# Second attention of a four-layer kernel: two PSUM banks for the products of maxima and three for those of exponents, in place of three and two

## The chip, the cores and the metric

The kernel runs on one core of one Trainium2 chip. The metric is the device time of one execution in microseconds. A core has TensorE (PE, whose weight loads have a row of their own, PEld), VectorE (DVE), ScalarE (ACT), GpSimd (POOL) and SyncE (SP, which only issues DMAs here). TensorE writes its results to PSUM, which this kernel uses as eight banks of 512 fp32 columns on 128 partitions; VectorE and ScalarE read them from there.

## What is computed

The input is x of shape (4, 512, 512). Four layers follow one another, each added to x: an attention with a learned sparse mask (`attn_a`), a feed-forward layer, a differential attention (`attn_b`), and the same feed-forward layer again. The change lies in `attn_b`, whose input is the layer-normed x:

```python
q1, k1, q2, k2 = ...            # (B, T, 16 heads, 16), slices of x @ W_attn
v = ...                         # (B, T, 16 heads, 32)
lam = exp(dot(lambda_q1, lambda_k1)) - exp(dot(lambda_q2, lambda_k2)) + LAMBDA_INIT
attn1 = einsum('bthd,bshd->bhts', q1, k1) * scale
attn2 = einsum('bthd,bshd->bhts', q2, k2) * scale
score = softmax(attn1 - lam * attn2, axis=-1)
out = einsum('bhts,bshd->bthd', score, v)
out = (1.0 - LAMBDA_INIT) * out.reshape(B, T, E)
return out @ W_proj
```

## The kernel before

The whole kernel is written by hand in Bass. Each engine has its own queue and runs it strictly in order; engines wait for one another through semaphores (`wait_ge`). The function `attention_b` (L1949) emits the second attention. It goes by 16 units (`UNITS`, L1826), each of four heads (`HU`) of one of four batches, four units to a batch. A unit has 16 tiles (`TILES`, L1827) of 128 rows by 512 columns.

The softmax is computed twice over. For the maxima, TensorE makes the product of a tile of 128 queries with all 512 keys (step `max_b`, L2117) into a bank of `O1_BANKS`, and VectorE reduces it to a maximum per query (L2220, `maxes_b`). When all 16 tiles of a unit are done, the maxima are transposed by TensorE (step `place_b`, L2124), copied by ScalarE (L2276) and placed by four DMAs as one more row of the stacked queries. For the exponents, TensorE then makes the transposed product, 128 keys by 512 queries, with the maximum already subtracted through that row (step `exp_b`, L2132), into a bank of `O2_BANKS`, and ScalarE takes its exponential (L2288, `ex_b`, a ring of ten buffers). GpSimd adds the exponentials of a unit up (L2070, `ex_sum`), in the last unit VectorE half of them. TensorE multiplies them with the values (step `weighted_b`, L2143, bank 5) and sums `ex_sum` over partitions (step `sums_b`, L2155). VectorE divides in eight pieces (step `divide_b`: a reciprocal, L2229, and a multiplication, L2230). The projection follows for each batch (step `project_b`, L2166, added to x in L2236).

Other steps run beside these through two side banks (6 and 7): the normed rows (`norm_b`, L2192) are transposed (`turn_b`, L2079, copied in L2255), and from these come values (`values_b`, L2090, copied in L2260) and queries and keys (`product_b`, L2102). The latter are split into a high half on ScalarE (L2270) and a low half on VectorE (L2212), and sent by SyncE through a DRAM buffer to the stacks (`send_b`, L2315 and L2319).

The order of all this is written out by `order_of_attention_b` (L1830), and every engine walks the same list and takes its own part of each step. It goes in slots: each holds one `exp_b` and one `max_b`, and behind these perhaps a `weighted_b` (every fourth), half of a side step, a `divide_b`, a `norm_b` or a `stats_b`. The exponents of unit n run `LAG` = 6 slots behind the maxima of unit n+1. A product of maxima waits until its bank has been read, and so does one of exponents:

```python
pe.wait_ge(max_made, i + 1 - len(O1_BANKS))   # L2116, i counts the tiles of maxima
pe.wait_ge(ex_made, i + 1 - len(O2_BANKS))    # L2131, i counts the tiles of exponents
```

The last batch is projected in steps `early_b` (L2178: three of four parts, as soon as there is a bank) and `last_b` (L2183), each of whose four tiles has a bank of `LAST_BANKS`; they are added to x in L2242. The first steps of the second feed-forward layer (`EARLY_FFN`, L1322) stand among them in the order. Its transposes (`turned`, L1497, banks 4 and 5) wait for all exponentials, and two of them stand ahead of the first `early_b` that the change touches.

Of the kernel before, what the change touches and what calls it, by code (L numbers as in the profile page):

```python
# [7 lines left out]
ACT = mybir.ActivationFunctionType  # L8
AX = mybir.AxisListType
# [6 lines left out]
P = 128  # L16
B, S, D = 4, 512, 512
NT = S // P
# [1930 lines left out]
def attention_b(k, mem):  # L1949
    nc, d, ps, x = k.nc, k.d, k.ps, k.x  # L1950
    pe, dve, act, pool, sp, chain = k.pe, k.dve, k.act, k.pool, k.sp, k.dve_chain
    signal = k.flag
    ROWS, N_EX, N_OUT, SCALE = 97, 10, UNITS_B + 1, HDB ** -0.5
    O1_BANKS, O2_BANKS, SUM_BANK, SIDE = (0, 1, 2), (3, 4), 5, (6, 7)
    LAST_BANKS = O1_BANKS + O2_BANKS[:1]
    order = order_of_attention_b()
    nth = numbered(order)
    small, qk_weights, v_weights, proj_weights = (
# [113 lines left out]
    def tensor(kind, *at):  # L2072
        step = (kind, *at)
        if kind == "turn_b":
            b, f = at
            pe.wait_ge(zb_made, NT * b + NT)
            side_free(step)
            for t in range(NT):
                s = nc.tensor.transpose(ps[:, side_bank[step], t * P:t * P + P], z[:, t, f * P:f * P + P],  # L2079
                                        k.ident[:, :])  # L2080
            s.then_inc(zb_turned, 1)
        elif kind == "values_b":
            b, t, half = at
            bank = side_bank[step[:3]]
            if half == 0:
                pe.wait_ge(zt_made, ND * b + ND)
                pe.wait_ge(v_weights, 16)
                side_free(step[:3])
            for f in range(2 * half, 2 * half + 2):
                s = nc.tensor.matmul(ps[:, bank, :], z_t[:, b % 2, f, t * P:t * P + P], w_v[:, f, :],  # L2090
                                     start=f == 0, stop=f == ND - 1)
            if half:
                s.then_inc(vb_done, 1)
        elif kind == "product_b":
            n, i, half = at
            b, c, bank = n // UNITS_B, n % UNITS_B, side_bank[step[:3]]
            if half == 0:
                pe.wait_ge(zt_made, ND * b + ND)
                pe.wait_ge(qk_weights, 16)
                side_free(step[:3])  # L2100
            for f in range(2 * half, 2 * half + 2):
                s = nc.tensor.matmul(ps[:, bank, :], w_qk[:, f, c, i, :], z_t[:, b % 2, f, :], start=f == 0,  # L2102
                                     stop=f == ND - 1)
            if half:
                s.then_inc(qk_done, 1)
        elif kind == "query_scale":
            pe.wait_ge(lam_made, 4)
            nc.tensor.matmul(ps[:, SUM_BANK, 0:1], q2_row[:, :], lam[:, 1:2], start=True,
                             stop=True).then_inc(lam_spread, 1)
        elif kind == "max_b":  # L2110
            n, j = at
            g, t = divmod(j, NT)
            i = TILES * n + j
            if j == 0:
                pe.wait_ge(stacked[n % 3], 16 * 6 * (n // 3 + 1))
            pe.wait_ge(max_made, i + 1 - len(O1_BANKS))  # L2116
            nc.tensor.matmul(ps[:, O1_BANKS[i % 3], :], q_stack[0:ROWS - 1, n % 3, g, t * P:t * P + P],  # L2117
                             k_stack[0:ROWS - 1, n % 3, g, :], start=True, stop=True).then_inc(max_in, 1)
        elif kind == "place_b":
            n, = at  # L2120
            pe.wait_ge(max_made, TILES * n + TILES)
            side_free(step)
            for t in range(NT):
                s = nc.tensor.transpose(ps[0:HU, side_bank[step], t * P:t * P + P], maxes[:, n % 2, :, t],  # L2124
                                        k.ident[:, :])
            s.then_inc(maxes_turned, 1)
        elif kind == "exp_b":
            n, t, g = at
            i = tile_at(n, t, g)
            pe.wait_ge(in_place[n % 2], 16 * HU * (n // 2 + 1))  # L2130
            pe.wait_ge(ex_made, i + 1 - len(O2_BANKS))  # L2131
            nc.tensor.matmul(ps[:, O2_BANKS[i % 2], :], k_stack[:, n % 3, g, t * P:t * P + P],  # L2132
                             q_stack[:, n % 3, g, :], start=True, stop=True).then_inc(exp_in, 1)
        elif kind == "weighted_b":
            n, t = at
            b, c = n // UNITS_B, n % UNITS_B
            pe.wait_ge(vb_made, NT * b + NT)
            pe.wait_ge(out_sums, n)
            pe.wait_ge(ones_made, 2)
            for g in range(HU):  # L2140
                i, first = tile_at(n, t, g), P * c + 32 * g
                pe.wait_ge(ex_made, i + 1)
                s = nc.tensor.matmul(ps[32 * g:32 * g + 32, SUM_BANK, :], v[:, b % 2, t, first:first + 32],  # L2143
                                     ex[:, i % N_EX, :], start=t == 0, stop=t == NT - 1)
            s.then_inc(weighted_done, 1)
        elif kind == "sums_b":
            n, = at
            if n < UNITS - 1:
                pe.wait_ge(ex_added, (TILES - HU) * (n + 1))
            else:  # L2150
                pe.wait_ge(ex_added, (TILES - HU) * n + (TILES - HU) // 2)
                pe.wait_ge(ex_added_last, (TILES - HU) // 2)
            side_free(step)
            for g in range(HU):
                s = nc.tensor.matmul(ps[32 * g:32 * g + 32, side_bank[step], :], ones[:, :], ex_sum[:, g, :],  # L2155
                                     start=True, stop=True)
            s.then_inc(sums_done, 1)
        elif kind == "project_b":
            b, t, half = at
            bank = side_bank[step[:3]]  # L2160
            if half == 0:
                pe.wait_ge(divided, 2 * NT * (UNITS_B * b + UNITS_B - 1) + 2 * t + 2)
                pe.wait_ge(proj_weights, 16)
                side_free(step[:3])
            for c in range(2 * half, 2 * half + 2):
                s = nc.tensor.matmul(ps[:, bank, :], out_t[:, (UNITS_B * b + c) % N_OUT, t * P:t * P + P],  # L2166
                                     w_proj[:, c, :], start=c == 0, stop=c == ND - 1)
            if half:
                s.then_inc(proj_done, 1)
        elif kind == "early_b":  # L2170
            t, = at
            pe.wait_ge(divided, 2 * NT * (UNITS - 1))
            pe.wait_ge(proj_weights, 16)
            pe.wait_ge(max_made, TILES * UNITS)
            if t == NT - 1:
                pe.wait_ge(ex_made, TILES * UNITS)
            for c in range(ND - 1):
                nc.tensor.matmul(ps[:, LAST_BANKS[t], :], out_t[:, (UNITS - UNITS_B + c) % N_OUT, t * P:t * P + P],  # L2178
                                 w_proj[:, c, :], start=c == 0, stop=False)
        elif kind == "last_b":  # L2180
            t, = at
            pe.wait_ge(divided, 2 * NT * (UNITS - 1) + 2 * t + 2)
            nc.tensor.matmul(ps[:, LAST_BANKS[t], :], out_t[:, (UNITS - 1) % N_OUT, t * P:t * P + P],  # L2183
                             w_proj[:, ND - 1, :], start=False, stop=True).then_inc(proj_done, 1)

    def vector(kind, *at):
        step = (kind, *at)
        if kind == "norm_b":
            b, t = at
# [24 lines left out]
        elif kind == "max_b":  # L2214
# [2 lines left out]
            i = TILES * n + j  # L2217
            dve.wait_ge(maxes_turned, n - 1)
            dve.wait_ge(max_in, i + 1)
            nc.vector.tensor_reduce(maxes[:, n % 2, g, t:t + 1], ps[:, O1_BANKS[i % 3], :], AX.X,  # L2220
                                    ALU.max).then_inc(max_made, 1)
        elif kind == "exp_b" and at[0] == UNITS - 1 and at[2] < HU // 2:
            add_exponentials(dve, nc.vector, ex_added_last, *at, HU // 2, 0)
# [25 lines left out]
    def scalar(kind, *at):  # L2249
# [33 lines left out]
        elif kind == "exp_b":  # L2283
            n, t, g = at
            i = tile_at(n, t, g)
            ex_free(i)
            act.wait_ge(exp_in, i + 1)
            nc.scalar.activation(ex[:, i % N_EX, :], ps[:, O2_BANKS[i % 2], :], ACT.Exp,  # L2288
                                 scale=SCALE).then_inc(ex_made, 1)
        elif kind == "weighted_b" and at[1] == NT - 1:  # L2290
            n, t = at
            act.wait_ge(weighted_done, NT * n + NT)
            if n >= N_OUT:
                act.wait_ge(proj_done, NT * ((n - N_OUT) // UNITS_B + 1))
            nc.scalar.activation(out_t[:, n % N_OUT, :], ps[:, SUM_BANK, :], ACT.Copy).then_inc(out_sums, 1)
        elif kind == "sums_b":
            n, = at
            act.wait_ge(sums_done, n + 1)
            act.wait_ge(divided, 2 * NT * n)
            nc.scalar.activation(sums_sb[:, :], ps[:, side_bank[step], :], ACT.Copy).then_inc(sums_made, 1)  # L2300
# [93 lines left out]
```

## Time and profile before

| | |
|---|---|
| median of 3 runs | 3121.16 us (3119.94 to 3121.54) |
| the profiled execution | 3118.84 us |
| its span, first to last instruction | 3117.6 us |
| mean granted clock of TensorE | 0.979 |
| PE, DVE, ACT, POOL busy | 2976.5, 2338.5, 1773.3, 1059.6 us |
| first product of maxima (L2117) | 2094.4 us |
| last product of exponents (L2132) | 2562.8 us |

The profile is of one execution. Times of rows are microseconds from the start of the span. TensorE's matmuls are pipelined and their ends are modelled, so that a busy PE is not PE at its peak; what holds it up is best read from the idle time before a row. In rows of the time order, the bracket at the end gives the idle time of the engine before that instruction and what ended it; "issue" is time in which it waited for nothing that the profile shows. The weight load (PEld) of a product carries its semaphore waits and stands ahead of it.

### The profile page before, as it was taken

Reading aid. Unit: us, or ns where it says so; the run is one execution under the profiler, and the core shown is the slowest. Engines: PE = TensorE matmul, PEld = TensorE weight load, DVE = VectorE, ACT = ScalarE, POOL = GpSimd, SP = SyncE. Lnnn points to the kernel's source line nnn. Section 1 sums busy time; section 2 is a strip of 40 time slices with the busy share of each in tenths; the row PEclk is TensorE's granted clock in tenths of the full one; section 3 lists DMA queues with packets and bytes.
Section 4 is the critical chain, followed back from the end, with each engine's and each line's share of the span. In section 5 each row is a group of like instructions: output and inputs, shape, how many; then the busy total and the mean of one; then the engine's idle time right before and its main releaser. Section 6 shows DMA issues by size and latency. Waiting matters only on the chain. (4 is left out here: it accounts for less than half of the span.)

```text
span 3117.6 us, 56883 instructions
## 1 busy us (share of the span) xinstructions
PE 2976.5 (95%) x22569; PEld 1808.2 (58%) x22569; DVE 2338.5 (75%) x4298; ACT 1773.3 (57%) x2896; POOL 1059.6 (34%) x881
## 2 busy tenths in 40 slices
PE   6999999999999999999899999989999988999999
PEld 3554445445568544444478778854444435787887
DVE  6998999999999887777366676655766776667665
ACT  4988888888889466666643333323443443334332
POOL 1000000000000454533255565613554555556653
PEclk9999999999999799999999999999999998999999
DMA  2000000000000000000112111133332321112211
GB/s 76 2 2 12 2 2 12 2 2 12 2 2 2 1 2 1 2 1 1 35 44 58 51 44 51 45 106 109 77 102 68 102 55 34 45 58 71 58 48 48
DMA packets 105805, 112.93 MB, mean 36 GB/s; under 512 B 8963, under 2 KB 74500, under 8 KB 105157
## 3 DMA queue, kind: packets, MB, share of 16 engines
q1 hardware_dynamic: 102918, 108.61, 12.5%
q8 instruction: 180, 2.95, 0.4%
q10 hardware_dynamic: 2624, 0.69, 0.1%
q14 instruction: 83, 0.68, 0.1%
HBM read 84.76 MB, written 20.97 MB: 34 GB/s over the span
## 5 line engine op out<-in xcount | busy, mean ns | idle before, releaser
L778 DVE TENSOR_SCALAR pair_in<-key_words,row_words 128x512 f32<-128x512 f32 x1792 | 726.1, 480 | 33.8 <-PE ps L664 30.0
L868 ACT ACTIVATE pair_mid<-ps,row_bias 128x512 f32<-128x512 f32 x896 | 589.3, 690 | 115.0 <-PE ps L664 97.5
L664 PE MATMUL ps<-pair_in,w_hi 128*32 128x512 f16 x7168 | 627.2, 391 | 11.6 <-DVE pair_in L778 11.2
L664 PE MATMUL ps<-pair_in,w_lo 128*32 128x512 f16 x3584 | 404.8, 390 | 0.0
L664 PEld LDWEIGHTS ps<-pair_in,w_hi 128*32 128x32 f16 x7168 | 268.2, 95 | 199.3 <-issue 33.6
L1121 DVE TENSOR_REDUCE maxes<-ps 128x2 f32<-128x1024 f32 x256 | 303.6, 1221 | 92.7 <-PE ps L1034 90.7
L896 POOL TENSOR_SCALAR_AFFINE_SELECT sim<-sim 128x512 f32<-128x512 f32 x15 | 9.6, 639 | 981.7 <-ACT sim L885 981.7
L1167 ACT ACTIVATE ex<-ps 128x512 f32<-128x512 f32 x448 | 243.2, 595 | 119.0 <-PE ps L1053 118.2
L1543 PE MATMUL ps<-ffn_b_hi,ffn_a_hi 128*128 128x512 f32 x904 | 286.0, 398 | 24.3 <-DVE ffn_up L1631 9.1
L1543 PE MATMUL ps<-ffn_b_lo,ffn_a_hi 128*128 128x512 f32 x904 | 283.0, 394 | 3.9 <-DVE ffn_b_lo L1613 3.9
L1543 PE MATMUL ps<-ffn_b_hi,ffn_a_lo 128*128 128x512 f32 x904 | 281.5, 393 | 0.7 <-POOL ffn_a_lo L1774 0.7
L1681 DVE TENSOR_TENSOR x<-x,ps 128x512 f32<-128x512 f32 x256 | 175.6, 686 | 135.0 <-PE ps L1560 132.1
L679 PE MATMUL ps<-pair_mid,w_slide 128*32 128x512 f32 x2048 | 248.9, 592 | 0.0
L2288 ACT ACTIVATE ex_b<-ps 128x512 f32<-128x512 f32 x256 | 146.7, 596 | 174.4 <-PE ps L2132 168.1
L2220 DVE TENSOR_REDUCE maxes_b<-ps 128x1 f32<-128x512 f32 x256 | 169.4, 682 | 85.0 <-PE ps L2117 84.3
L1543 PEld LDWEIGHTS ps<-ffn_b_hi,ffn_a_hi 128*128 128x128 f32 x904 | 169.4, 190 | 69.7 <-DVE ffn_up L1631 11.7
L1774 POOL TENSOR_TENSOR ffn_a_lo<-ffn_sums,ffn_a_hi 128x1024 fp32r<-128x1024 f32 x60 | 148.1, 2468 | 170.7 <-ACT ffn_a_hi L1696 170.7
L1543 PEld LDWEIGHTS ps<-ffn_b_lo,ffn_a_hi 128*128 128x128 f32 x904 | 171.6, 190 | 42.0 <-DVE ffn_b_lo L1613 5.8
L1741 ACT ACTIVATE ffn_gate<-ffn_gate 128x512 f32<-128x512 f32 x60 | 37.9, 632 | 275.7 <-DVE ffn_gate L1638 275.7
L1543 PEld LDWEIGHTS ps<-ffn_b_hi,ffn_a_lo 128*128 128x128 f32 x904 | 171.8, 190 | 37.7 <-POOL ffn_a_lo L1774 1.2
L664 PEld LDWEIGHTS ps<-pair_in,w_lo 128*32 128x32 f16 x3584 | 137.2, 95 | 85.5 <-issue 25.1
L2070 POOL TENSOR_TENSOR ex_sum<-ex_sum,ex_b 128x512 f32<-128x512 f32 x124 | 156.7, 1281 | 82.4 <-ACT ex_b L2288 82.3
(247 smaller groups left out, 5436.4 us busy)
## 6 DMA issues: line engine op xcount, KB each, us to landing
ffn_raw_up<-in_w_ffn SPq DMA_DIRECT2D x64, 512.0 KB, 4.0
ffn_raw_down<-in_w_ffn SPq DMA_DIRECT2D x64, 256.0 KB, 2.7
q_stack<-halves SPq DMA_DIRECT2D x48, 256.0 KB, 5.1
k_stack<-halves SPq DMA_DIRECT2D x48, 256.0 KB, 5.9
halves<-hi_b SPq DMA_DIRECT2D x16, 512.0 KB, 2.7
halves<-lo_b SPq DMA_DIRECT2D x16, 512.0 KB, 3.6
out<-x SPq DMA_DIRECT2D x4, 1024.0 KB, 4.5
x<-in_x SPq DMA_DIRECT2D x6, 512.0 KB, 6.0
```

The source lines that it names most:

```text
L664: s = nc.tensor.matmul(ps[32 * quarter:32 * quarter + 32, bank + which, :], w_part[:, at_w:at_w + 32], words.rearrange("p (s two) -> p s t ...
L679: s = nc.tensor.matmul(ps[32 * c:32 * c + 32, 6 + w, :], p.w3_slide[:, 30 - 2 * r:62 - 2 * r], p.pair_mid[:, n % NG, half, :], start=r == ...
L778: s = nc.vector.tensor_scalar(p.pair_in[:, (4 * n + i) % N_PAIR, :], p.key_words[:, b % 2, :], p.row_words[:, b % 2, row:row + 1], None, A ...
L868: nc.scalar.activation(p.pair_mid[:, n % NG, which, :], ps[:, bank + which, :], ACT.Relu, bias=bias).then_inc(p.mid_made, 1)
L1121: nc.vector.tensor_reduce(maxes[:, c % 2, 2 * pair:2 * pair + 2, h], ps[:, 2 * pair:2 * pair + 2, :], AX.X, ALU.max).then_inc(maxes_made, 1)
L1167: nc.scalar.activation(ex[:, i % N_EX, :], ps[:, EXP_BANKS[j], :], ACT.Exp, scale=2.0 ** -0.5).then_inc(ex_made, 1)
L1543: i = nc.tensor.matmul(bank, a_part[:, s % 2, a_at, h, :], b_part[:, place(operand), h, :], start=opens and (which, m, h) == (0, 0, 0), st ...
L1681: nc.vector.tensor_tensor(x[:, n, :], x[:, n, :], ps[:, 6 + t % 2, :], ALU.add).then_inc(x_added, 1)
L1774: nc.gpsimd.tensor_tensor(lo, source, hi.bitcast(F32), ALU.subtract).then_inc(w_lo_made, 1)
L2070: engine.tensor_tensor(ex_sum[:, g, :], first, ex[:, i % N_EX, :], ALU.add).then_inc(done, 1)
L2220: nc.vector.tensor_reduce(maxes[:, n % 2, g, t:t + 1], ps[:, O1_BANKS[i % 3], :], AX.X, ALU.max).then_inc(max_made, 1)
L2288: nc.scalar.activation(ex[:, i % N_EX, :], ps[:, O2_BANKS[i % 2], :], ACT.Exp, scale=SCALE).then_inc(ex_made, 1)
```

## The change

It moves one of five PSUM banks from the products of maxima to those of exponents. Bank 2 changes its owner, and three places that had the counts 3 and 2 written out take the lengths of the tuples. The last projection keeps the banks 0 to 3; its tiles from the third on, where before only the fourth did, wait for all exponentials.

```diff
-    O1_BANKS, O2_BANKS, SUM_BANK, SIDE = (0, 1, 2), (3, 4), 5, (6, 7)
-    LAST_BANKS = O1_BANKS + O2_BANKS[:1]
+    O1_BANKS, O2_BANKS, SUM_BANK, SIDE = (0, 1), (2, 3, 4), 5, (6, 7)
+    LAST_BANKS = O1_BANKS + O2_BANKS[:2]
...
-            nc.tensor.matmul(ps[:, O1_BANKS[i % 3], :], q_stack[0:ROWS - 1, n % 3, g, t * P:t * P + P],
+            nc.tensor.matmul(ps[:, O1_BANKS[i % len(O1_BANKS)], :], q_stack[0:ROWS - 1, n % 3, g, t * P:t * P + P],
...
-            nc.tensor.matmul(ps[:, O2_BANKS[i % 2], :], k_stack[:, n % 3, g, t * P:t * P + P],
+            nc.tensor.matmul(ps[:, O2_BANKS[i % len(O2_BANKS)], :], k_stack[:, n % 3, g, t * P:t * P + P],
...
-            if t == NT - 1:
+            if t >= len(O1_BANKS):
                 pe.wait_ge(ex_made, TILES * UNITS)
...
-            nc.vector.tensor_reduce(maxes[:, n % 2, g, t:t + 1], ps[:, O1_BANKS[i % 3], :], AX.X,
+            nc.vector.tensor_reduce(maxes[:, n % 2, g, t:t + 1], ps[:, O1_BANKS[i % len(O1_BANKS)], :], AX.X,
...
-            nc.scalar.activation(ex[:, i % N_EX, :], ps[:, O2_BANKS[i % 2], :], ACT.Exp,
+            nc.scalar.activation(ex[:, i % N_EX, :], ps[:, O2_BANKS[i % len(O2_BANKS)], :], ACT.Exp,
```

## Rows read from the trace of the kernel before

**Rows 1.** Table of stretches: busy us of PE, PEld, DVE, ACT, POOL (instructions), granted clock, DMA.

```profile
2122.00:2188.00 66.00, 65.15 (x263) 30.34 (x261) 39.88 (x67) 32.20 (x59) 34.12 (x28) 1.00 0.31 80
2188.00:2312.00 124.00, 117.85 (x450) 53.27 (x449) 87.49 (x154) 51.04 (x93) 61.01 (x49) 0.99 0.33 86
2312.00:2433.00 121.00, 115.16 (x447) 52.03 (x445) 85.76 (x150) 50.81 (x92) 60.06 (x48) 1.00 0.34 88
...
2520.00:2542.00 22.00, 18.24 (x78) 6.81 (x78) 20.64 (x35) 11.99 (x22) 16.51 (x14) 0.92 0.21 58
```

**Rows 2.** Waits from 2094 to 2566 us: who waited for whom, total, times, longest.

```profile
PEld ps L2132 <- ACT ex_b L2288: 37.0, 55, 2.6
...
PEld ps L2117 <- DVE maxes_b L2220: 11.4, 28, 1.7
PE ps L2132 <- ACT ex_b L2288: 10.4, 15, 2.2
...
PE ps L2117 <- DVE maxes_b L2220: 4.8, 8, 1.3
```

**Rows 3.** Groups by line, 2094 to 2566 us: count, busy us, mean ns, idle before.

```profile
L2220 DVE TENSOR_REDUCE maxes_b<-ps 128x1 f32<-128x512 f32 x256 | 169.4, 682 | 85.0 <-PE ps L2117 84.3
...
L2230 DVE TENSOR_TENSOR out_t<-out_t,sums_sb 128x64 f32<-128x64 f32 x120 | 69.2, 577 | 4.1
L2229 DVE RECIPROCAL sums_sb<-sums_sb 128x64 f32<-128x64 f32 x120 | 64.8, 540 | 10.1 <-ACT sums_sb L2300 10.1
```

**Rows 4.** Time order, start of unit 8: start, us, instruction, idle before and what ended it.

```profile
2311.63 0.40 PE L2117 MATMUL ps<-k_stack,q_stack 96*128 96x512 f32 x1
...
2311.87 0.40 PE L2132 MATMUL ps<-q_stack,k_stack 97*128 97x512 f32 x1
...
2312.67 0.47 PE L2117 MATMUL ps<-k_stack,q_stack 96*128 96x512 f32 x1 [0.40 <-DVE maxes_b L2220]
...
2314.29 0.68 DVE L2220 TENSOR_REDUCE maxes_b<-ps 128x1 f32<-128x512 f32 x1
```

**Rows 5.** Time order, end of unit 10 and start of 11: a burst behind VectorE's idle time.

```profile
2399.29 0.69 DVE L2220 TENSOR_REDUCE maxes_b<-ps 128x1 f32<-128x512 f32 x1 [1.95 <-PE ps L2117]
...
2403.26 0.68 DVE L2220 TENSOR_REDUCE maxes_b<-ps 128x1 f32<-128x512 f32 x1
...
2403.99 0.19 PEld L2117 LDWEIGHTS ps<-k_stack,q_stack 96*128 96x128 f32 x1 [0.19 <-DVE maxes_b L2220]
...
2405.60 0.19 PEld L2117 LDWEIGHTS ps<-k_stack,q_stack 96*128 96x128 f32 x1 [1.30 <-issue]
...
2406.95 1.28 DVE L2220 TENSOR_REDUCE maxes_b<-ps 128x1 f32<-128x512 f32 x2
```

**Rows 6.** Time order, unit 9, tile 6, and the first projection behind.

```profile
2351.07 0.19 PEld L2117 LDWEIGHTS ps<-k_stack,q_stack 96*128 96x128 f32 x1
...
2352.22 2.47 DVE L2220 TENSOR_REDUCE maxes_b<-ps 128x1 f32<-128x512 f32 x4
...
2358.63 1.55 PE L2166 MATMUL ps<-wb_proj,out_t 128*128 128x512 f32 x3 [1.11 <-DVE out_t L2230]
```

**Rows 7.** Time order, unit 8: TensorE idle for a low half, an exponential, a DMA.

```profile
2320.15 1.98 PE L2102 MATMUL ps<-zb_t,wb_qk 128*128 128x512 f32 x4 [1.01 <-DVE lo_b L2212]
...
2331.96 0.50 PE L2132 MATMUL ps<-q_stack,k_stack 97*128 97x512 f32 x1 [0.47 <-ACT ex_b L2288]
...
2339.32 0.50 PE L2117 MATMUL ps<-k_stack,q_stack 96*128 96x512 f32 x1 [1.27 <-DMA k_stack<-halves]
```

**Rows 8.** Time order, GpSimd: first and last sums of unit 14's exponentials.

```profile
2534.40 1.28 POOL L2070 TENSOR_TENSOR ex_sum<-ex_b 128x512 f32<-128x512 f32 x1 [4.33 <-ACT ex_b L2288]
...
2546.66 3.72 POOL L2070 TENSOR_TENSOR ex_sum<-ex_sum,ex_b 128x512 f32<-128x512 f32 x3 [0.88 <-ACT ex_b L2288]
```

**Rows 9.** Table of stretches around a fall of the clock, columns as in rows 1.

```profile
2214.00:2216.00 2.00, 0.35 (x2) 0.14 (x2) 1.97 (x4) 0.93 (x2) 2.00 (x3) 1.00 0.30 55
...
2218.00:2220.00 2.00, 2.00 (x5) 1.05 (x4) 0.62 (x2) 0.19 (x1) 0.47 (x1) 0.50 0.00 0
```

## The prediction

> **What bounds the kernel now.** The second attention is 472 us of the 3117.6 us span. I read the table of stretches first [rows 1]. TensorE is busy for 115 of 121 us between 2312 and 2433 us and for 65 of 66 us between 2122 and 2188, at a granted clock of 1.00: the middle of the stage goes by TensorE's own queue. Its end does not, with 18.2 of 22 us from 2520 on. VectorE has 86 of the same 121 us, ScalarE 51. So of the two engines that empty the banks, VectorE has 1.7 times the work, and it is the one that loses a bank here.
>
> The table of waits says who holds TensorE up [rows 2]. "PEld" is the weight load in front of a product; its idle time begins when the load before it is over, while that load's product still streams, so it overstates a stall, and the idle time of PE itself understates one. ScalarE's exponentials: 37.0 us on the loads (55 times), 10.4 on PE (15 times). VectorE's maxima: 11.4 (28 times) and 4.8 (8 times). The change pays for relief from the larger row with the smaller. That is its case, and the rows must show whether it holds.
>
> The groups of instructions [rows 3]: a maximum takes 0.68 us, 256 of them. VectorE's queue holds 120 reciprocals of 0.54 us and 120 multiplications of 0.58 us on the mean between the maxima. A product that nothing holds starts 0.24 us after the one before (2311.63 and 2311.87, rows 4). Where a slot of the written order holds only one exponential's product and one maximum's, TensorE needs about 0.5 us, VectorE 0.68 us plus half a division (0.56), 1.2 us in all. There TensorE runs ahead and the number of maxima banks says by how far. Where a slot holds half a side step too (1.98 us for its four passes, rows 7), TensorE needs over 2 us and VectorE catches up. The stage alternates between the two kinds, about twice in a unit.
>
> **What the change does, part by part.**
>
> *Maxima, three banks to two.* The product of tile i waits for the reduction of tile i-2 in place of i-3. The price at a tile is the end of the reduction two tiles back less the start of the load, plus 0.05 us: a reduction that ended at 2403.94 let a load start at 2403.99 [rows 5]. I worked it out tile by tile for units 8 to 11, which took 2312.6 to 2433.7 us; units 4 to 7 look the same (their stretch in rows 1 has nearly the same busy times). There are six bursts in which a product would start too early. Three of them stand in the rows:
> - Unit 8, tile 0 starts at 2312.67, held by the reduction three back, and would wait for the one that starts at 2314.29 and ends at 2314.97: 2.4 us [rows 4].
> - Unit 9, tile 6 loads at 2351.07; the reduction two back is the first of four that start at 2352.22, and ends at 2352.90: 1.9 us [rows 6].
> - Unit 11, tile 0 loads at 2405.60; the reduction two back starts at 2406.95 and ends at 2407.63: 2.1 us [rows 5].
> - The other three, of the same pattern, come to 1.3 us (unit 8, tile 6), 1.4 us (unit 8, tile 14) and 0.9 us (unit 9, tile 10).
>
> Within one burst delays don't add, since VectorE's queue is full there and doesn't move; I take the largest. Between bursts VectorE runs dry and is fed by TensorE (1.95 us idle before 2399.29, rows 5), so it moves with it and the next burst's delay comes on top. Together 10.0 us for four units.
>
> *What gives it back.* A TensorE that comes later finds waits gone that don't hang on it. The clearest are its own idle times: 1.01 us for a low half on VectorE at 2320.15, 1.27 us for the DMA of the stacks at 2339.32 [rows 7], 1.11 us for a division at 2358.63 [rows 6]: 3.4 us. The exponentials' waits go too: one of 0.47 us at 2331.96 [rows 7], and an estimated 1 us in smaller ones of the same kind, 10.4 us over the stage [rows 2] being 2.7 us for four units and most of it in the last ones: 1.5 us. Net 10.0 - 4.9 = 5.1 us for four units.
>
> *Exponentials, two banks to three.* The product of tile i waits for the exponential of i-3. At most this gives back the 10.4 us of idle PE for certain and 37.0 us by the loads. I take only the 1.5 us per four units above. Both kinds of product stand alternately in one queue, so a product released earlier meets the maximum's product behind it sooner, and that waits on the slower engine. At 2312.67 TensorE is idle for a maximum, not for an exponential [rows 4].
>
> *The last two units.* GpSimd's sums of the exponentials of unit 14 start at 2534.40, take 1.28 us each and end at 2550.4; twelve of them are 15.4 of these 16.0 us [rows 8]. The exponentials' stalls are largest here, but those sums decide: the one hole in them that an exponential explains is 0.88 us. I take 0 (bounds -2, for that hole and as much behind it, to 0). What TensorE has lost before 2534 is kept, since it shifts the first of these sums.
>
> *The final projection.* LAST_BANKS names banks 0 to 3 before and after. Its third tile now waits for all exponentials too, but the transposes of the feed-forward stage stand before it in the queue and wait for them already: 0. Without that cover it would cost what the last exponential is late at the third tile, which comes behind a whole sum over partitions and six passes of the projection.
>
> *Sum.* Four groups of four units. The first is lighter: unit 0 has no exponentials beside it, and in units 1 to 3 TensorE is busy for 65 of 66 us and VectorE for only 40 [rows 1]. I count it half: 3.5 x 5.1 = 18 us. Against the profiled execution, 3118.8 us, this is 3136.8. The median of the runs lies 2.3 us above that execution, so 3139.1; I say 3139.0.
>
> **What speaks against it, and the rivals.** A measurement of this kernel can tell about 0.2%, 6.2 us, from no change.
>
> *A, forecast: VectorE's bursts hold TensorE, 10 to 28 us longer* (3131 to 3149). The lower end is 2.5 us per group, half my net; the upper one 8 us for each of 3.5 groups, if only the low halves' waits give anything back.
>
> *B, given back: within 6.2 us.* A late TensorE is absorbed by whatever it waits for next, and my 4.9 us is a reading of the large waits alone. If units 8 to 11 absorb 8.5 of the 10.0 us, 3.5 x 1.5 = 5 us remain: 3126. For it: the three waits of 1.0 to 1.3 us [rows 6, 7] stand between the bursts, where a delay meets them. Against it: TensorE's own idle time is 5.8 us of 121 [rows 1], of which I have counted most.
>
> *C, the exponentials were the true limit: faster.* It decides in the bursts, from the point at which VectorE is done with tile i-2 before ScalarE is done with exponential i-2. Then the 10.4 us of idle PE go and most maxima don't bind: with 2 us of maxima that still bind, 10.4 - 2 = 8 us gained, 3113. At 2331.96 this is so [rows 7]; at the three places shown it is not. The Trainium skill (Perfetto Trace Analysis, Optimization Strategies) says to go for the engine that the matmul engine waits for, and by the totals of rows 2 that is ScalarE, which would speak for the change. What the trace shows is that the totals are of waits at different places.
>
> *D, the clock falls oftener: 28 to 45 us longer.* The granted clock fell to 0.50, 1.2 GHz, in 2218 to 2220, behind a stretch from 2214 to 2216 in which TensorE was busy for 0.35 of 2 us [rows 9]. Its row lacks 1.0 us of full clock and the stage's stretch with 0.99 lacks 1.2 to 1.9 us, say 1.6, and my new holes are of 1 to 2.4 us each. Seven more such falls would bring 11 us on top of 18: 3150. The Trainium skill (TensorE: Matmul & The Clock Gate, A second HAM failure mode: psum-queue depth-cycling) tells of a kernel that cycled through PSUM banks, idled briefly between groups and so lost throughput to a clock that kept dropping. The trace here shows one such fall in 121 us at most (0.99 and 1.00 in the two long stretches of rows 1), so I give it little.
>
> That the change doesn't do what it says can be left out: the counts and the choice of bank follow the lengths of the two tuples everywhere.
>
> **How the numbers follow.** A 0.60, B 0.22, C 0.08, D 0.10. Predicted is A's 3139. For 8 in 10 I leave out C, the part of B below 3121 and what of D lies above 3158: 3120 to 3158. Faster by over 0.2% (below 3114.9): 0.07, nearly all of C. Within: 0.21, B less a little. Slower (above 3127.4): 0.72, of A and D and the rest of B.
>
> **What would show it.** Right: TensorE's waits for exponentials fall below 15 us on loads outside the last unit, those for maxima rise from 11.4 to over 30 us; the stage from the first maximum's product (2094.4) to the final projection (2566.4) becomes some 18 us longer, the groups of units 4 to 7 and 8 to 11 each by about 5; VectorE's and ScalarE's busy times and all other stages stay. Wrong, for B: new waits for maxima of 30 us, but those for low halves, divisions and DMA nearly gone and the stage equally long. For C: waits for maxima hardly grow. For D: more stretches below 1.00. It would be wrong too if VectorE's multiplications, 0.58 us on the mean but of unequal length, came out longer or shorter in the bursts, since a shift of the queues by 2 us changes which of them stands where.

## The result: 24 us slower

| | before | after |
|---|---|---|
| median | 3120.84 us (4 runs) | 3144.49 us (4 runs, 3141.39 to 3148.13) |
| ratio to before | | 1.0078, 95% interval 1.0064 to 1.0092 |
| profiled execution, its span | 3118.84, 3117.6 us | 3148.13, 3146.9 us |
| mean granted clock of that execution | 0.979 | 0.974 |
| PE, DVE, ACT, POOL busy | 2976.5, 2338.5, 1773.3, 1059.6 | 2990.7, 2336.7, 1771.6, 1059.0 |

The forecast was 3139.0 us with a range of 3120 to 3158, slower with a chance of 0.72. The profiled execution after is the slowest of its four, 3.6 us above their median, so that its rows show some 29 us where the medians differ by 24.

All of it lies in the second attention. The tables of stretches of both kernels, first the kernel before from its first product of maxima to the final projection, and its last four units:

```profile
2094.00:2566.00 472.00, 440.72 (x1680) 195.93 (x1680) 332.56 (x573) 199.41 (x358) 234.93 (x186) 0.98 0.35 89
...
2433.90:2566.40 132.50, 115.96 (x459) 47.11 (x457) 104.13 (x182) 61.58 (x109) 79.06 (x63) 0.96 0.28 72
```

and the changed kernel: units 4 to 11, units 12 to 15, the whole stage (columns as in rows 1).

```profile
2191.50:2450.90 259.40, 239.40 (x896) 108.63 (x896) 170.46 (x302) 101.26 (x185) 121.62 (x96) 0.97 0.32 82
...
2450.90:2596.70 145.80, 125.46 (x459) 51.06 (x457) 102.53 (x177) 60.94 (x109) 76.77 (x61) 0.87 0.26 66
...
2092.00:2597.00 505.00, 458.51 (x1681) 203.02 (x1680) 331.78 (x574) 198.44 (x358) 235.06 (x186) 0.94 0.32 84
```

VectorE, ScalarE and GpSimd do the same work (331.8, 198.4 and 235.1 us against 332.6, 199.4 and 234.9). The stage is 32 us longer in these two executions. By the starts of the first product of maxima of every fourth unit in the time order, units 0 to 3 take 98.7 us instead of 94.4, units 4 to 7 130.8 instead of 123.8, units 8 to 11 128.6 instead of 121.2, and the rest 145.8 instead of 132.5. The granted clock of the last four units fell from 0.96 to 0.87.

The waits of the changed kernel from 2092 to 2597 us, which answer to rows 2 (who waited for whom, total us, times, longest):

```profile
PEld ps L2117 <- DVE maxes_b L2220: 54.7, 59, 2.5
...
PE ps L2117 <- DVE maxes_b L2220: 33.8, 33, 2.0
...
PEld ps L2102 <- DVE lo_b L2212: 10.9, 13, 0.8
PEld ps L2132 <- ACT ex_b L2288: 6.7, 9, 0.8
...
PEld ps L2166 <- DVE out_t L2230: 4.6, 5, 1.2
PEld ps L2117 <- DMA k_stack<-halves: 3.7, 2, 2.1
...
PE ps L2132 <- DMA q_stack<-max_t_b: 2.5, 1, 2.5
...
PE ps L2132 <- ACT ex_b L2288: 0.6, 2, 0.3
```

The third bank of exponents did what it was there for: TensorE's idle time for them went from 10.4 to 0.6 us. The second bank of maxima had to pay: from 4.8 to 33.8 us. Net, TensorE's own idle time for the two grew by 19.2 us, and its busy time in the stage by 17.8 us (440.72 to 458.51) for the same 1680 products, at the lower clock. Two of the places at which it now stands, in time order (unit 9, tile 6, then unit 10, tile 14):

```profile
2363.27 1.97 DVE L2220 TENSOR_REDUCE maxes_b<-ps 128x1 f32<-128x512 f32 x3
2364.00 0.19 PEld L2117 LDWEIGHTS ps<-k_stack,q_stack 96*128 96x128 f32 x1 [2.46 <-DVE maxes_b L2220]
...
2415.24 2.49 POOL L2070 TENSOR_TENSOR ex_sum<-ex_b 128x512 f32<-128x512 f32 x2 [0.93 <-ACT ex_b L2288]
2415.46 1.13 DVE L2230 TENSOR_TENSOR out_t<-out_t,sums_sb 128x64 f32<-128x64 f32 x1
2416.51 0.68 DVE L2220 TENSOR_REDUCE maxes_b<-ps 128x1 f32<-128x512 f32 x1
...
2417.24 0.19 PEld L2117 LDWEIGHTS ps<-k_stack,q_stack 96*128 96x128 f32 x1 [2.26 <-DVE maxes_b L2220]
```

In both the weight load starts 0.05 us after the end of a reduction: at 2363.27 the first of three, of 0.68 us each, ends at 2363.95. In rows 6 the load of unit 9, tile 6 had gone 1.8 us ahead of that reduction's end. At 2415.46 a multiplication of 64 columns takes 1.13 us and pushes the reduction behind it; the row of GpSimd (POOL) above it matters further down.

### The profile page after: what moved, and what is told of

It reads as the page before. It is cut to its first block and busy times, and to the rows that moved or that the text cites. A ratio compares the mean times of both kernels' runs of the same rounds, so it can differ in the third digit from the quotient of the medians.

```text
span 3146.9 us, 56868 instructions
## 1 busy us (share of the span) xinstructions
PE 2990.7 (95%) x22569; PEld 1817.4 (58%) x22569; DVE 2336.7 (74%) x4298; ACT 1771.6 (56%) x2896; POOL 1059.0 (34%) x881
```

## Experiments

All times are medians; ratios are to the kernel before, with their 95% interval in brackets. "m3_e2" stands for three banks of maxima and two of exponents (before), "m2_e3" for the changed kernel, and so on.

### The two halves of the change apart

Only the loss of a bank (m2_e2):

```diff
-    O1_BANKS, O2_BANKS, SUM_BANK, SIDE = (0, 1), (2, 3, 4), 5, (6, 7)
-    LAST_BANKS = O1_BANKS + O2_BANKS[:2]
+    O1_BANKS, O2_BANKS, SUM_BANK, SIDE = (0, 1), (3, 4), 5, (6, 7)
+    LAST_BANKS = (0, 1, 2, 3)
```

> Two banks for the maxima and two for the exponents, bank 2 unused: only the half of the change that takes a bank away. Theory A (VectorE's bursts hold TensorE when the maxima have two banks; the third bank of exponents is worth little): as slow as the changed kernel or a little slower, 22 to 32 us over the kernel before. Rival (the third bank of exponents, by releasing its products earlier, is itself the cause, since it fills VectorE's and GpSimd's queues in another order): within 6 us of the kernel before.

Measured: 3146.19 us, ratio 1.0084 (1.0069 to 1.0099), 26 us over the kernel before and 2 us over the changed one, within the intervals. Its waits from 2092 to 2600 us:

```profile
PEld ps L2117 <- DVE maxes_b L2220: 43.8, 53, 2.0
...
PE ps L2117 <- DVE maxes_b L2220: 27.7, 36, 1.6
...
PEld ps L2132 <- ACT ex_b L2288: 25.6, 39, 2.7
```

So the loss of the maxima's bank alone makes the whole result. With two banks of exponents TensorE itself is idle for 27.7 us for maxima and 6.5 for exponentials; with three (the changed kernel) for 33.8 and 0.6. Both add up to 34 us: the wait moved from one product to the one behind it in the same queue. (m2_e2 keeps the changed wait of the last projection; that this costs nothing is read from the traces below.)

Only the gain of a bank. The kernel uses all eight of its banks, so the side steps had to do with one. The three lines of banks are those of the base (m3_e2_side1), of the test (m3_e3_side1) and, with the free bank on the other side, of m4_e2_side1, whose LAST_BANKS are (0, 1, 2, 7):

```diff
-    O1_BANKS, O2_BANKS, SUM_BANK, SIDE = (0, 1), (2, 3, 4), 5, (6, 7)
-    LAST_BANKS = O1_BANKS + O2_BANKS[:2]
+    O1_BANKS, O2_BANKS, SUM_BANK, SIDE = (0, 1, 2), (3, 4), 5, (6,)
+    O1_BANKS, O2_BANKS, SUM_BANK, SIDE = (0, 1, 2), (3, 4, 7), 5, (6,)
+    O1_BANKS, O2_BANKS, SUM_BANK, SIDE = (0, 1, 2, 7), (3, 4), 5, (6,)
+    LAST_BANKS = (0, 1, 2, 3)
...
-            bank = SIDE[len(side_bank) % 2]
+            bank = SIDE[len(side_bank) % len(SIDE)]
```

> The base of the next two: the kernel before with one side bank (6) in place of two, bank 7 unused; nothing is left out. Side steps wait for the copy of the one before: 10 to 60 us over the kernel before.

> One side bank, three banks for the maxima and three for the exponents (bank 7 is the third): the other half of the change alone. Theory A (the third bank of exponents is worth little): 0 to 4 us below m3_e2_side1. Theory C (ScalarE's exponentials hold TensorE, and with three banks for the maxima the relief would show): 8 us or more below it.

> One side bank, four banks for the maxima and two for the exponents: the freed bank on the maxima's side. Theory A (TensorE runs ahead of VectorE by as many products as there are banks): some more of the waits for maxima goes, 3 to 12 us below m3_e2_side1. Rival (three are enough): within 3 us of it.

Measured: 3174.95, 3172.66 and 3177.71 us, ratios 1.0169 (1.0151 to 1.0187), 1.0163 (1.0145 to 1.0180) and 1.0178 (1.0162 to 1.0194). The third bank of exponents gives 2 us and a fourth bank of maxima costs 3, neither clear of the intervals, which are some 5 us to either side: the 8 us that the rival asked for did not come, but these four and five runs place the gain no closer than several microseconds. The waits for maxima and exponentials, first of the base, then of m3_e3_side1:

```profile
PEld ps L2132 <- ACT ex_b L2288: 33.2, 50, 2.6
...
PEld ps L2117 <- DVE maxes_b L2220: 12.2, 30, 1.7
...
PE ps L2132 <- ACT ex_b L2288: 8.6, 13, 2.2
...
PE ps L2117 <- DVE maxes_b L2220: 4.9, 8, 1.3
```

```profile
PEld ps L2117 <- DVE maxes_b L2220: 17.3, 39, 1.7
...
PE ps L2117 <- DVE maxes_b L2220: 6.5, 11, 1.3
PEld ps L2132 <- ACT ex_b L2288: 6.5, 8, 0.8
```

Here nothing is taken from the maxima, the exponentials' 8.6 us of idle time vanish, and the time stays within the noise. The fourth bank of maxima misses its expected 3 to 12 us: three are enough here, although TensorE's idle time for maxima still fell from 4.9 to 2.7 us. What these three kernels don't settle is whether it is the same with two side banks, since one side bank alone costs 53 us.

### What makes two banks too few

The theory behind the forecast was VectorE's work between the maxima. First the divisions were cut to one column, with three and with two banks of maxima (this leaves the division of the softmax out):

```diff
+            part = slice(part.start, part.start + 1)
             chain(nc.vector.reciprocal(sums_sb[:, part], sums_sb[:, part]))
```

> The kernel before, with the reciprocals and multiplications of the divisions cut from 64 columns to one, so that the softmax's division is left out and VectorE has some 110 us less work in the stage; all instructions and waits stay. Theory A: TensorE's waits for maxima fall to nearly nothing, and the time falls by 3 to 12 us against the kernel before, most of it where TensorE waits for divisions and maxima.

> The changed kernel with the same cut: the division is left out. Theory A (the divisions between the maxima make the bursts in which two banks are too few): within 6 us of m3_e2_short_div. Rival (two banks are too few for the product, the reduction and the handing back alone, 0.5 + 0.68 us): still 15 us or more over m3_e2_short_div.

Measured: 3112.07 us (0.9972, 0.9962 to 0.9981) and 3132.47 us (1.0042, 1.0027 to 1.0056). The second expectation failed: 20 us between the two, not under 6, as many as the rival asked for. The reason stands in the rows of m2_e3_short_div. Group and time order:

```profile
L2231 DVE TENSOR_TENSOR out_t<-out_t,sums_sb 128x1 f32<-128x1 f32 x120 | 76.9, 641 | 4.3 <-DVE sums_sb L2230 0.2
L2230 DVE RECIPROCAL sums_sb<-sums_sb 128x1 f32<-128x1 f32 x120 | 18.2, 151 | 13.5 <-ACT sums_sb L2301 13.5
```

```profile
2413.16 3.74 POOL L2070 TENSOR_TENSOR ex_sum<-ex_sum,ex_b 128x512 f32<-128x512 f32 x3
...
2414.51 1.16 DVE L2231 TENSOR_TENSOR out_t<-out_t,sums_sb 128x1 f32<-128x1 f32 x1
...
2415.60 0.68 DVE L2220 TENSOR_REDUCE maxes_b<-ps 128x1 f32<-128x512 f32 x1
```

The reciprocals shrank from 540 to 151 ns, but a multiplication of one column takes 641 ns on the mean, more than the 577 ns of one of 64 columns in rows 3. The one at 2414.51 ends at 2415.67; GpSimd's three sums of 1.25 us end at 2414.41, 2415.66 and 2416.90. It is not work: it stands until GpSimd's current sum is over. The whole trace bears this out. Of the 128 multiplications in m2_e3_short_div 50 take 0.16 us; the other 78, 0.92 us on the mean, all end 14 to 22 ns after an instruction of GpSimd has ended. In the kernel before, with 64 columns, 61 take 0.23 us on the mean; the other 67, 0.86 us on the mean, all end 79 to 88 ns after one. So over half of the multiplications that the forecast had counted as work were held by some 0.6 us each. The Trainium skill (SBUF — State Buffer, SBUF: two separate sides) says that VectorE and GpSimd share a pair of SBUF ports under an exclusive lock, and that an operation of VectorE with two SBUF inputs blocks until a GpSimd operation that reads SBUF is over. The trace agrees for the multiplication, which has two such inputs; the reciprocal, which has one, took 144 to 164 ns every time in m2_e3_short_div.

So the cut had left most of the burst in place. The next pair cuts the sums on GpSimd too (this leaves the softmax's denominator out):

```diff
-        first = ex[:, tile_at(n, 0, g) % N_EX, :] if t == 1 else ex_sum[:, g, :]
-        engine.tensor_tensor(ex_sum[:, g, :], first, ex[:, i % N_EX, :], ALU.add).then_inc(done, 1)
+        first = ex[:, tile_at(n, 0, g) % N_EX, 0:1] if t == 1 else ex_sum[:, g, 0:1]
+        engine.tensor_tensor(ex_sum[:, g, 0:1], first, ex[:, i % N_EX, 0:1], ALU.add).then_inc(done, 1)
```

Both kernels of the pair also fill `ex_sum` with ones once, on GpSimd ahead of the stage, since most of it is no longer written.

> The kernel before with one column in place of 64 in the divisions (as m3_e2_short_div) and one in place of 512 in the sums of exponentials, so that the softmax's denominator is left out. In m3_e2_short_div the multiplications of one column still took 0.64 us on the mean and often ended together with a sum on GpSimd. Theory A2 (VectorE's multiplications are held by GpSimd's sums, and this makes the bursts): the multiplications fall to 0.16 us each; the time falls by 10 to 30 us against the kernel before, since the last units don't wait for the sums either.

> The changed kernel with the same two cuts. Theory A2 (what stands between the maxima on VectorE, and how long GpSimd holds it, makes two banks too few): within 6 us of m3_e2_short_both. Rival (product, reduction and handing back alone are too much for two banks, whatever else VectorE does): 15 us or more over m3_e2_short_both, and waits for maxima as large as in the changed kernel.

Measured: 3099.50 us (0.9933, 0.9921 to 0.9945) and 3107.95 us (0.9956, 0.9945 to 0.9968): 8 us between the two, against 24 with everything in place. The multiplications and the waits for maxima of m2_e3_short_both:

```profile
L2233 DVE TENSOR_TENSOR out_t<-out_t,sums_sb 128x1 f32<-128x1 f32 x120 | 19.3, 160 | 4.3 <-DVE sums_sb L2232 0.2
```

```profile
PEld ps L2119 <- DVE maxes_b L2222: 32.1, 50, 2.0
...
PE ps L2119 <- DVE maxes_b L2222: 9.3, 14, 1.6
```

The multiplication falls to 160 ns, as expected, and TensorE's idle time for maxima to 9.3 us from 33.8. That is two thirds of the price gone with the divisions and the hold; the 8 us left are a little over the 6 expected. Product, reduction and handing back alone are thus not what costs 24 us, though 50 loads still wait. The sums cut alone, with whole divisions, were not run, so that the times don't tell the hold from the divisions' own length.

| maxima/exponents | stage, 3/2 | stage, 2/3 | medians differ by |
|---|---|---|---|
| nothing cut | 472.0 us | 503.9 us | 24 us |
| divisions cut | 467.3 us | 483.2 us | 20 us |
| divisions and sums cut | 459.3 us | 460.6 us | 8 us |

The stage is read from one execution each, from the first product of maxima to the first of the final projection. In the last row it differs by 1 us while the medians differ by 8. The two profiled executions differ by 8 too, 4.0 us of it ahead of the stage (it begins at 2093.5 and 2097.5 us) and 2.4 behind. In the middle row also 4.2 us lie ahead of it, and the stage itself has lost half of its price, where the medians show a sixth. Nothing that differs within a pair stands ahead of the stage, yet it began anywhere from 2090.6 to 2097.7 us in the kernels with two side banks. So single profiles can't place a few microseconds, and how much of the price went with the first cut and how much with the second stays open; that most of it went with both is shown by the medians and the profiles alike.

### Divisions in other slots

The burst should also shrink when the divisions leave the slots in which TensorE is quick:

```diff
-        if divisions and (i % 2 or n % UNITS_B == 1):
+        if divisions and (i < 6 or i in (9, 13) or n % UNITS_B == 1 or n >= UNITS - 1):
```

> The kernel before with six of the eight divisions of a unit moved into slots 0 to 5, which hold side steps, and two left in slots 9 and 13 (in three of four units; the units with projections keep their order); nothing is left out. Theory A: VectorE has less between the maxima in the plain slots, and the time falls by 0 to 6 us.

> The changed kernel with the same order of divisions; nothing is left out. Theory A: what two banks cost shrinks where the divisions left the plain slots, from 24 us over the kernel before to 8 to 18 us over m3_e2_spread. Rival (the divisions have nothing to do with it): still 24 us over m3_e2_spread.

Measured: 3121.89 us (1.0007, 0.9999 to 1.0015) and 3143.38 us (1.0076, 1.0064 to 1.0088). With three banks nothing is gained; with two the price is 21 us, 2.5 us less and not the 6 or more expected. In units 4 to 11 a part of the theory shows: two banks cost 10.9 us there (253.6 against 242.7 us) where they cost 14.5 in the plain order (259.5 against 245.0). But the last unit of m3_e2_spread takes 55.9 us instead of 46.5. Its stretch:

```profile
2513.20:2569.10 55.90, 44.87 (x148) 14.86 (x148) 37.41 (x66) 23.11 (x42) 30.25 (x24) 0.66 0.10 26
```

The granted clock is 0.66 there (0.91 in the kernel before), and its edit also moved the divisions of unit 14 closer together. Which of the two lengthened it was not tried. The pair is weak evidence: moving the divisions may only move the burst, since multiplications still meet sums of GpSimd there (58 of 128 are held in m2_e3_spread, 66 in the changed kernel).

### Multiplications on GpSimd

If GpSimd holds VectorE's multiplications, they might as well stand in its own queue, with three banks of maxima:

```diff
+            if n < UNITS - 2:
+                nc.vector.reciprocal(sums_sb[:, part], sums_sb[:, part]).then_inc(recip_made, 1)
+                return
...
+        if kind == "divide_b" and at[0] < UNITS - 2:
+            n, piece = at
+            part, out = slice(piece * P // 2, piece * P // 2 + P // 2), out_t[:, n % N_OUT, :]
+            pool.wait_ge(recip_made, 2 * NT * n + piece + 1)
+            pool.wait_ge(out_sums, n + 1)
+            nc.gpsimd.tensor_tensor(out[:, part], out[:, part], sums_sb[:, part], ALU.mult).then_inc(divided, 1)
```

> The kernel before with the multiplications of the divisions of units 0 to 13 on GpSimd in place of VectorE; nothing is left out. If VectorE's multiplications are slow because GpSimd's sums hold them, VectorE loses some 65 us of work and all the holding, GpSimd gets 112 short multiplications more: waits of TensorE for maxima fall from 16 us to under 6 us, and the time falls by 2 to 10 us. If GpSimd becomes late instead (its sums and multiplications in one queue, each waiting for VectorE's reciprocals), the time rises by up to 10 us.

Measured: 3124.18 us, ratio 1.0012 (1.0002 to 1.0021), 3 us slower. From its waits and groups, 2097 to 2575 us:

```profile
PEld ps L2156 <- POOL ex_sum L2071: 12.9, 8, 3.0
...
PE ps L2156 <- POOL ex_sum L2071: 9.3, 8, 2.5
...
PEld ps L2118 <- DVE maxes_b L2221: 8.0, 20, 1.7
...
PE ps L2118 <- DVE maxes_b L2221: 3.0, 5, 1.3
```

```profile
L2313 POOL TENSOR_TENSOR out_t<-out_t,sums_sb 128x64 f32<-128x64 f32 x112 | 35.8, 320 | 116.1 <-DVE sums_sb L2231 111.5 <-ACT ex_b L2293 4.5
```

The waits for maxima fell from 11.4 and 4.8 us to 8.0 and 3.0. But GpSimd's queue runs in order, each multiplication waits there for a reciprocal, the sums of exponentials behind it come later, and TensorE now idles 9.3 us for them, where the kernel before idled 0.2 us at most. The second of the two outcomes came.

### The clock

In m2_e2 bank 2 is free, so TensorE could be given spare products in the holes:

```diff
+            if j >= 10 or j in (5, 6):
+                nc.tensor.matmul(ps[:, 2, :], q_stack[0:ROWS - 1, n % 3, g, t * P:t * P + P],
+                                 k_stack[0:ROWS - 1, n % 3, g, :], start=True, stop=True)
             pe.wait_ge(max_made, i + 1 - len(O1_BANKS))
```

> As m2_e2, with a spare product of 0.24 us into the unused bank 2 ahead of the product of maxima in 8 of the 16 tiles of each unit (tiles 5, 6 and 10 to 15, where TensorE waits for VectorE), 128 in all, 31 us of TensorE work. Theory D (a good part of the loss is the clock that falls in TensorE's new holes): fewer stretches at half clock in the stage than the changed kernel's 68 us, and a time equal to m2_e2 or below it by up to 8 us. Theory A without D (the loss is waiting alone): the spare products that stand where TensorE doesn't wait cost their time, 5 to 20 us over m2_e2, whatever the clock does.

Measured: 3147.28 us, ratio 1.0081 (1.0066 to 1.0096), 1 us over m2_e2. The whole stage, first of m2_e2, then of m2_e2_filled:

```profile
2096.60:2600.00 503.40, 463.52 (x1680) 202.25 (x1680) 330.33 (x573) 200.80 (x358) 235.41 (x186) 0.93 0.32 84
```

```profile
2096.60:2596.00 499.40, 468.44 (x1808) 219.96 (x1808) 332.15 (x573) 202.00 (x358) 235.47 (x186) 0.98 0.33 84
```

With 128 products more, an estimated 31 us of work at 0.24 us each, the clock of the stage rises from 0.93 to 0.98, back to that of the kernel before, and TensorE is idle for 31 us of it in place of 40. So the falls do come with the holes. The time is the same within the intervals: the 5 to 20 us over m2_e2 that waiting alone would have brought did not come. How much the clock gave back can't be read from this pair, since what the spare products cost by themselves was not measured.

How much of the 24 us is clock can be estimated from all runs. The full clock that an execution lacks is its time multiplied by one less its mean granted clock. Within the 136 runs of these fourteen kernels, each against the mean of its own kernel, a microsecond more of lacking clock goes with 0.39 us more time (correlation 0.73). The kernel before lacks 61.9 us on the mean of 51 runs, the changed one 74.7 on 4, m2_e2 77.4 on 5. So 12.8 us lacking, at 0.39, are 5 us of the 24, and the waiting is 19. This is an estimate and not a shown split: the 0.39 comes from chance differences between executions, in which longer waits may lower the clock as well as the other way round. The profiles allow a larger share, since of the 32 us by which the stage grew TensorE's busy time makes 17.8.

## Why the prediction was right, step by step

The cause was right, shown by m2_e2. That the number came within 6 us is in part luck: the terms below were partly too small and the clock was left out of the sum.

*What bounds the stage, and who is the slower reader:* right. The totals of waits spoke for ScalarE (37.0 and 10.4 against 11.4 and 4.8 us, rows 2), the places spoke for VectorE, and m2_e2 and m3_e3_side1 show that the places were the better guide: a third bank against the exponentials' larger total was worth about 2 us, within the noise.

*The price of the lost bank, 10.0 us for four units, counted where a product would start before the reduction two tiles back had ended:* the bursts were right, and so, nearly, was their price. Over units 4 to 11 the waits for maxima grew by 15.2 us of idle PE, which understates a stall, and by 20.6 us on the loads, which overstate it; twice 10.0 were forecast. At the places of the list idle PE shows 0.9 us for unit 8, tile 6 (1.3 forecast), 1.2 for tile 14 (1.4), 2.0 for unit 9, tile 6 (1.9) and 0.4 for tile 10 (0.9). The other two bursts mostly hold TensorE a tile or two earlier: 1.8 us fell on unit 10, tile 14, and only 0.6 on unit 11, tile 0, and at the start of unit 8 there were 1.6 us, with 1.2 at tiles 13 and 14 before it. One place was not in the list, unit 11, tile 14, with 1.0 us.

Net, units 4 to 7 grew by 7.0 us and units 8 to 11 by 7.4, where 5.1 each were forecast. Of these 14.4 us TensorE's idle time of all kinds makes 8.4, under the forecast 10.2; the other 6.0 are its busy time, which grew from 233.4 to 239.4 us. The clock goes with it: over the eight units the changed kernel has 0.97 where the kernel before had 0.99 and 1.00, some 6.5 us more lacking, by the 0.39 above 2.5 us of time.

*What gives it back, 4.9 us for four units:* somewhat too much. TensorE's other idle times fell by 6.8 us over units 4 to 11, where twice 4.9 were forecast. Of these 0.8 us in each group were exponentials and not 1.5; the DMA's 1.27 us at the start of unit 9 did not go. By the loads, waits on weight loads for low halves fell from 13.8 to 10.9 us over the stage, for divisions from 7.7 to 4.6, for the DMA of the stacks from 6.7 to 3.7: 9 us over the stage, where 3.4 for each of 3.5 groups are 12.

*The first group at half, 2.5 us:* 4.3 measured. *The last two units, 0 beyond the shift, and the last group like the others:* this was the term furthest off. The last group grew by 13.3 us, not 5.1. Unit 12 alone went from 25.3 to 30.9 us and unit 15 with the tail from 46.5 to 50.6. In unit 15 GpSimd's sums did not decide alone: the waits for exponentials went, but waits for maxima (3.3 us) and one of 2.5 us for the DMA that places the last maxima came in their place, and the clock there fell from 0.91 to 0.81. Over the whole last group the changed kernel lacks 0.13 x 145.8 = 19 us of full clock against 0.04 x 132.5 = 5, and at 0.39 this is an estimated 5 us of it. The other 3 us stay with waiting.

*The final projection, 0:* no cost shows. From its first product to the end of the span the kernels take 551.2 and 549.9 us.

*The sum, 18 us:* the waiting came to 19 by the estimate of the clock's share above, so that by it the forecast was near for its own mechanism; over the profile's groups it is 32 - 0.39 x (0.06 x 505 - 0.02 x 472) = 24 us, in an execution that was itself 4 us slow. What was missing from the sum is D, the clock: it was held for a rival of 0.10 that would add 11 us, and came in at an estimated 5, as a part of the result beside A and not in place of it. The new idle times of up to 2.0 us on TensorE go here with a granted clock of 0.94 in the stage in place of 0.98. The Trainium skill (TensorE: Matmul & The Clock Gate, A second HAM failure mode: psum-queue depth-cycling), named for it there, tells of such a case, brief idling between groups and a clock that drops; the trace agrees in kind. *Rivals B and C* forecast no change and a faster kernel, and fall with the 24 us; m3_e3_side1 speaks against C besides, and the small sizes of what was given back against B. The lower end of A, 2.5 us for each of 3.5 groups, is 9 us and not 10, which changes nothing.

*What made the bursts* was only half understood. The forecast took VectorE's divisions for work, 0.56 us for half of one; that over half of the multiplications' time was a wait for GpSimd was not seen, though their unequal length (0.22 to 1.36 us) was noticed. The bursts' sizes came out all the same because they rested on rows of starts and ends, which contain the hold.

## What to carry to other kernels

Totals of waits per engine say which resource is waited for, not which is worth more: where two kinds of product alternate in one queue, the wait for one hides that for the other (34 us in both kernels with two banks of maxima, whatever the exponents had). Count instead, at each place, how late the release would be with one buffer fewer, take the largest of a burst and add over the bursts. Give the deeper ring to the reader whose queue also holds other and uneven work, as here VectorE's, and allow for the clock on top (here an estimated 5 of 24 us). Where an instruction of one kind is of unequal length, look what runs on the other engines when the long ones end.

## What the runs showed of the hardware

A VectorE multiplication of two SBUF operands with one column took 641 ns on the mean beside GpSimd's 512-column sums, and 160 ns when those were cut to one column. It takes its own time or stands until a GpSimd instruction ends: with one column all 78 long ones of m2_e3_short_div ended 14 to 22 ns after one, with 64 columns all 67 long ones of the kernel before 79 to 88 ns after one (0.86 us on the mean, against 0.23 us for the others). Cutting such an instruction from 64 columns to one brought nothing in the held ones; the profile shows the hold as busy time of VectorE. Mean granted clock and time of one and the same kernel go together: the fastest run of the kernel before took 3114.6 us at 0.982, the slowest 3128.6 us at 0.977.
